# Sixteen delta-memory heads in groups of four instead of two, with feature maps built in place and betas and output weights streamed

## What is computed

```python
# B, S, D = 2, 2048, 256;  H, DK, DV = 16, 128, 128;  SEG = 64 (32 segments)
q, k, v = x @ Wq, x @ Wk, x @ Wv            # x: layer-normed, split in heads and segments
beta = sigmoid(betas)                        # [1, H, 1, DV]
for each segment:                            # carry: mem [B,H,DK,DV], z [B,H,DK,1]
    sigma_q = elu(qq) + 1;  sigma_k = elu(kk) + 1
    att_dot = softmax(causal(qq @ kk.T / sqrt(DK))) @ vv
    att_mem = sigma_q @ mem / (sigma_q @ z)
    delta   = vv - sigma_k @ mem / (sigma_k @ z)
    mem += sigma_k.T @ delta;  z += sum(sigma_k)
    out = (beta * att_mem + (1 - beta) * att_dot) @ Wo
x = x + out
x = x + experts(layernorm(x)) + shared(layernorm(x))
```

## Time and profile before

| | us |
|---|---|
| median of 3 runs (lowest, highest) | 1780.19 (1779.05, 1781.97) |
| the profiled execution, its own time | 1777.83 |
| its span, first to last instruction | 1776.1 |
| TensorE busy | 1719.9 |
| VectorE busy | 1167.2 |
| ScalarE busy | 923.3 |
| GpSimd busy | 534.3 |
| mean granted TensorE clock | 0.996 of full |

### The profile page before, as it was taken

One profiled execution on the slowest core, in us unless ns is written; L12 is line 12 of the kernel. 1 busy time (PEld: TensorE's weight loads), 2 busy tenths in 40 slices (PEclk: granted clock), 3 DMA queues, 4 the chain that ended last, 5 costly groups with the idle time before them and its releaser, 6 DMA issues.

```text
span 1776.1 us, 45751 instructions
## 1 busy us (share of the span) xinstructions
PE 1719.9 (97%) x17966; PEld 1469.0 (83%) x17966; DVE 1167.2 (66%) x4020; ACT 923.3 (52%) x2192; POOL 534.3 (30%) x566
## 2 busy tenths in 40 slices
PE   5899999999999999999999999999999999998998
PEld 5788888888888888888888888888888888885555
DVE  6756757575766757575767757575757767587554
ACT  4655646464655646464646546464646556452130
POOL 2332323232323323232323323232323323230251
PEclk9999999999999999999999999999999999998999
DMA  4200000100000000100000000101000000125947
GB/s 156 72 22 26 15 20 8 33 8 15 26 15 26 16 20 8 33 8 15 26 15 26 16 20 8 33 8 30 11 15 26 15 26 9 30 73 174 293 87 213
DMA packets 83238, 75.07 MB, mean 42 GB/s; under 512 B 21184, under 2 KB 73872, under 8 KB 82768
## 3 DMA queue, kind: packets, MB, share of 16 engines
q1 hardware_dynamic: 79664, 66.32, 12.4%
q0 software_dynamic: 3328, 5.81, 1.7%
q10 hardware_dynamic: 32, 0.01, 0.0%
HBM read 47.72 MB, written 24.40 MB: 41 GB/s over the span
## 4 chain that ended last, share of the span: by engine, by line
PE 90%; DVE 4%; ACT 3%; issue 2%; DMA 1%; SPq 0%; DVEq 0%; ACTq 0%
PE bank_o L1455 13%; PE bank_k L1350 12%; PE bank_q L1350 11%; PE bank_v L1360 9%; PE chain_k L1409 7%; PE chain_k L1399 7%; PE chain_q L1399 6%; PE bank_s L1373 4%; PE bank_a L1426 4%; PE bank_a L1436 3%; PE bank_s L1444 2%; PE bank_k L1382 2%; ACT step_place L657 1%; PE bank_q L1505 1%; PE bank_s L1524 1%
## 5 line engine op out<-in xcount | busy, mean ns | idle before, releaser
L517 POOL TENSOR_TENSOR step_place<-step_place 128x512 f32<-128x512 f32 x128 | 169.8, 1327 | 667.2 <-ACT step_place L657 667.2
L671 ACT ACTIVATE step_place<-chain_q,step_place 128x128 f32<-128x128 f32 x512 | 161.1, 372 | 258.9 <-DVE step_place L903 258.8
L919 DVE TENSOR_TENSOR step_place<-step_place,chain_k 128x258 f32<-128x258 f32 x255 | 107.5, 422 | 277.3 <-PE chain_q L1409 277.3
L1455 PE MATMUL bank_o<-step_place 128*128 128x256 f32 x1024 | 227.8, 381 | 0.9 <-ACT step_place L685 0.9
L1455 PEld LDWEIGHTS bank_o<-step_place 128*128 128x128 f32 x1024 | 193.4, 191 | 26.7 <-issue 1.3
L1409 PE MATMUL chain_k<-step_place 64*128 64x129 f32 x1020 | 180.8, 297 | 2.3 <-DVE step_place L909 2.2
L1409 PE MATMUL chain_q<-step_place 64*128 64x129 f32 x1020 | 180.8, 297 | 0.0
L1399 PE MATMUL chain_k<-step_place 128*64 128x129 f32 x2048 | 165.0, 281 | 10.6 <-DVE step_place L919 10.6
L1409 PEld LDWEIGHTS chain_k<-step_place 64*128 64x128 f32 x1020 | 131.9, 186 | 44.9 <-issue 42.2
L550 POOL TENSOR_TENSOR step_place<-step_place 128x256 f32<-128x256 f32 x128 | 78.5, 613 | 297.4 <-DVE step_place L1112 297.4
L526 POOL TENSOR_TENSOR step_place<-step_place 128x512 f32<-128x512 f32 x128 | 165.4, 1293 | 0.0
(11 more groups left out here) (204 smaller groups left out, 4212.6 us busy)
## 6 DMA issues: line engine op xcount, KB each, us to landing
expert_place<-in_L_ffn_w_dram SPq DMA_DIRECT2D x24, 512.0 KB, 7.5
expert_sums<-zero SPq DMA_DIRECT2D x16, 272.0 KB, 5.1
expert_rows<-w_in SPq DMA_DIRECT2D x15, 288.0 KB, 2.3
step_place<-in_L_attn_x_dram SPq DMA_DIRECT2D x16, 256.0 KB, 2.8
x_res<-in_L_attn_x_dram SPq DMA_DIRECT2D x16, 256.0 KB, 3.2
x_rows<-w_in SPq DMA_DIRECT2D x16, 256.0 KB, 2.1
x_normed_t<-x1t SPq DMA_DIRECT2D x16, 256.0 KB, 2.1
shared_place<-x_normed_t SPq DMA_DIRECT2D x8, 512.0 KB, 4.1
```

Source lines behind the costliest of these rows:

```text
L517: nc.gpsimd.tensor_tensor(vb[:, :, :, :].rearrange("p s j d -> p s (j d)"), val[:, :, :, :].rearrange("p s j d -> p s (j d)"), rows.unsque ...
L671: ins = nc.scalar.activation(am[:, par, seg, j, :], chain_q[:, j * ZC:j * ZC + DK], ACT.Copy, scale=rdq[:, seg, j:j + 1])
L919: ins = nc.vector.tensor_tensor(m, m, (chain_k, chain_q)[b][:, 0:HG * ZC].rearrange("p (j z) -> p j z", j=HG), ALU.subtract)
L1455: ins = mm(bank_o[:, b * D:(b + 1) * D], att[:, b * PIECES + i, :], wo[:, i, :], start=(i == 0 and b == 0), stop=(i == PIECES - 1), skip_g ...
```

## The change

Groups have four heads (HG = 4), so there are four groups in a block and 64 in all. A projection of keys or queries takes two banks (`bank_p[0]`, `bank_p[1]`) of two heads each, and each half has its own semaphore counts; values of one segment are projected with 512 columns into one bank, bank_a for seg 0 and bank_v for seg 1. The fourth head's memory chain does not fit in the banks of the others: it has `chain_3` and, for b = 1 of an update, a piece of `bank_s`. `attend` now has its loops in the order seg, head, b.

The exponentials of keys and queries are written where the feature map will stand, and the feature map is formed in place; betas times values are written where the delta will stand; normalized probabilities overwrite the scores. Only the betas of one group lie in SBUF and only half of Wo (eight pieces): SyncE loads betas once a group and each pair of Wo's pieces in every block, after the pair in its place has been used. Weights land directly where their low parts will be formed, without a landing buffer. The transposes of x, the transposed layer norm, `project_out`, logits and picks use bank_v and bank_a in place of bank_o. `project_out` runs in one piece after `numerators(n, g, 1)` of g = 0. The steps of layer norm and gate are put into four groups in place of eight.

```diff
-HG = 2
+HG = 4
-STEP_PLACE = 23760
+STEP_PLACE = 24545
...
+    def chain(kind, j):
+
+        if j == H3:
+            return chain_3, kind * ZC
+        return (chain_k, chain_q)[kind], j * ZC
+
+    def change(b, j):
+
+        if j == H3:
+            return (chain_3, bank_s)[b][:, 0:ZC]
+        return (chain_k, chain_q)[b][:, j * ZC:(j + 1) * ZC]
...
+        def load_betas(n):
+
+            if n:
+                sp.wait_ge(s["vb_ready"], 2 * n)
...
+        def load_wo(blk, c):
+
+            done = H // WC * (blk - 1) + c + 1 - WR // WC
+            if done > 0:
+                sp.wait_ge(s["wo_used"], done)
...
+            load_betas(n + 1)
             if first:
+                load_x(1)
                 for g in range(2, NG):
                     load_w(g)
...
+                for c in range(WR // WC, H // WC):
+                    load_wo(blk, c)
+                for c in range(WR // WC):
+                    load_wo(blk + 1, c)
+                store_x1(blk)
+                zero_part(blk)
...
         blocks(sp, body)
-        sp.wait_ge(s["v_mm"], NT)
+        for c in range(WR // WC, H // WC):
+            load_wo(NBLK, c)
+        sp.wait_ge(s["v_mm"], 2 * NT)
...
     @block.scalar body:
-                read_out(n, par, 0)
+                read_out(n, 0)
+                if nxt:
+                    for h in range(2):
+                        keys(n + 1, h)
                 act.wait_ge(s["s_shifted"], n + 1)
...
                 if nxt:
-                    queries(n + 1)
+                    for h in range(2):
+                        queries(n + 1, h)
+                if g == 1 and not first:
+                    side_x1t(blk)
+                if g == 2 and not last:
+                    x_turn(blk + 2)
+                read_out(n, 1)
+                if nxt:
+                    values(n + 1, 0)
                 act.wait_ge(s["pt_mm"], n + 1)
...
     @block.vector body:
+                if n:
+                    attended(n - 1)
+                delta(n, 0)
                 dve.wait_ge(s["s_mm"], n + 1)
...
+                if nxt:
+                    sigma_k(n + 1, 0)
+                state_last(n, g, 0)
+                if nxt:
+                    sigma_k(n + 1, 1)
+                state(n, g, 0)
...
+                delta(n, 1, nxt)
+
+                if nxt:
+                    for h in range(2):
+                        sigma_q(n + 1, h)
+                if first and g + 2 < NG:
+                    for i in range(3):
+                        split_lo(g + 2, i)
...
+                if g == 1 and not last:
+                    x_newton(blk + 2, 0, NEWTONS)
+                    x_apply()
                 if g == 2 and not first:
+                    gate_group_sums(blk)
+                    gate_groups(blk)
+                    gate_best(blk)
...
     @block.tensor:
+        def project_v(seg, g):
+            parts = [(w, x, c) for w, x in ((w_hi, xt_hi), (w_hi, xt_lo), (w_lo, xt_hi))
+                     for c in range(NC)]
+            for i, (w, x, c) in enumerate(parts):
+                ins = mm(seg_bank[seg][:, :], x[:, c, seg, :], w[:, g, 2, c, :],
+                         start=i == 0, stop=i == len(parts) - 1)
+            ins.then_inc(s["v_mm"], 1)
...
+            for seg in range(2):
+                pe.wait_ge(s["vo_ready"], 2 * n + seg + 1)
+                if more:
+                    pe.wait_ge(s["v_ready"], 2 * (n + 1) + seg + 1)
                 for j in range(HG):
                     for b in range(B):
...
                         half = b if seg == 0 else 1 - b
-                        ins = mm((bank_a, bank_v)[seg][ROWS[half], j * DK:(j + 1) * DK],
+                        ins = mm(seg_bank[seg][ROWS[half], j * DK:(j + 1) * DK],
                                  pt[ROWS[b], j, seg, :], vo[ROWS[b], seg, j, :],
                                  start=True, stop=True)
...
+                    for h in range(2):
+                        pe.wait_ge(s["ksig_ready"], 2 * n + h + 1)
+                        project_t(h, gn, 1).then_inc(s["k_mm"], 1)
...
+                if n:
+                    attended_transposes(n - 1)
                 update(n, 0)
                 if nxt:
+                    for h in range(2):
+                        pe.wait_ge(s["k_sig"], 2 * (n + 1) + h + 1)
+                        project_t(h, gn, 0).then_inc(s["q_mm"], 1)
...
+                numerators(n, g, 1)
+                if n:
+                    pe.wait_ge(s["att_ready"], 2 * n)
+                if g == 0 and not first:
+                    project_out(blk, n)
...
+                if nxt:
+                    project_v(0, gn)
                 probability_transposes(n)
                 if nxt:
+                    project_v(1, gn)
+                    for h in range(2):
+                        key_transposes(n + 1, h)
...
                 if nxt:
                     update(n, 1)
                 attend(n, nxt)
                 if nxt:
                     scores(n + 1, False)
```

More of the change, by code:

```diff
@@ L179, in layer @@
     kraw = take([128, HG, 2, B, SEG])
-    ex_q = take([128, HG * 2 * B * SEG])
-    ex_k = take([128, HG * 2 * B * SEG])
     val = take([128, 2, HG, DK])
-    vb = take([128, 2, HG, DK])
+    dl = [take([128, HG, ZC]) for seg in range(2)]
     vo = take([128, 2, HG, DK])
@@ L191, in layer @@
     pt = take([128, HG, 2, SEG])
[L192 to L195 removed]
+    am = [take([128, 2, HG, DK]), take([128, 1, HG, DK])]
+    rd = take([128, 2, 2 * HG])
     mask = take([128, SEG])
@@ L547, in body @@
                 nxt = not (last and g == NG - 1)
-                start = first and g == 0
                 pool.wait_ge(s["s_max"], n + 1)
@@ L697, in _ @@
                              ).then_inc(s["gwt_ready"], 1)
-        split_hi(1)
-        keys(0, True)
-        queries(0, True)
-        values(0, True)
-        key_rows(0, True)
+        for seg in range(2):
+            values(0, seg)
+        for h in range(2):
+            queries(0, h)
+        for i in range(3):
+            split_hi(1, i)
+        for h in range(2):
+            key_rows(0, h)
         def body(blk, first, last):
@@ L726, in body @@
-                read_out(n, par, 1)
+                                     bank_s[:, :], ACT.Copy).then_inc(s["pt_ready"], 1)
+                if nxt:
+                    values(n + 1, 1)
                 if first and g + 2 < NG:
-                    split_hi(g + 2)
-                if g == 3 and not first:
-                    side_x1t(blk)
-                if g == 4 and not first:
+                    for i in range(3):
+                        split_hi(g + 2, i)
+                if g == 1 and not first:
@@ L913, in delta, with state_last @@
             ins.then_inc(s["dl_ready"], 1)
+        def state_last(n, g, seg):
+            dve.wait_ge(s["upd_mm"], 2 * n + seg + 1)
+            for b in range(B):
+                m = mem[:, HG * g + H3, b, :]
+                ins = nc.vector.tensor_tensor(m, m, change(b, H3), ALU.subtract)
+            ins.then_inc(s["mem3_ready"], 1)
         def state(n, g, seg):
@@ L1637, in body @@
                     update(n, 1)
+                if g == 1 and not first:
+                    pe.wait_ge(s["lg_exp"], blk)
+                if g == 3 and not first:
+                    pe.wait_ge(s["pickv_ready"], blk + 1)
                 attend(n, nxt)
```

720 lines of the change are left out of this document (358 added, 362 removed).

## The result

| | median us | fast runs against before | 95% interval |
|---|---|---|---|
| before | 1780.26 | | |
| after | 1783.93 (1780.82 to 1788.71) | 1.0022 | 1.0016 to 1.0029 |

The forecast was 1713 us, the range 1652 to 1770. The changed kernel is 4 us slower, by 0.2%, and lies outside the range on the other side of no change.

A forecast was written before the change was run, and what follows sets the result against it. TensorE's instruction stream was the bound. A four-head group at 19.87 us (20.82 for two old) gave start 27, first block 86.3, 14 blocks 1335.6, last 98, rest 162: span 1709, median 1713, range 1652 to 1770.

The forecast's parts named there:

- the extra steps by group: VectorE's added steps in group 2 end at 19.1 us, some 0.3 late a block at most; group 0's residual covered.
- The first block: First block takes 86.3 us (95.20 before): four groups of 19.87, plus 0.4 and 6.4.
- Stage edges (1): TensorE's 1.53 us a group between stages is paid 64 times in place of 128: -98 us.
- Rival D: TensorE's stage edges grow with the heads: +98 us, 1811; chance 0.03.
- Attend (2): Attend's segment-by-segment order keeps two tiles working at a time: +0.87 us a group, +56 us.
- Rival A: TensorE overlaps attend over both segments, as four tiles do before the change: -56 us, 1657; chance 0.10.
- Values (3): Values projection: 12 matmuls of 512 columns at 0.216 us replace 24 of 256: -0.29 us a group, -18 us.
- E: Two row tiles writing one bank take turns in attend, 3.46 us a group: +111 us, 1824; chance 0.02.
- The loop through feature maps: Other engines' chain from numerators to query maps ends at 14.6 us, asked at 14.9: no TensorE wait.
- B: Loop through VectorE and ScalarE costs 0.3 to 1.1 us a group more: 1725 to 1775, middle 1750; chance 0.22.
- C: Loop from numerators to key transposes is 1.4 us or more longer; at 2 us longer, 1822; chance 0.08.
- Streaming of Wo and betas: Reloads are hidden: Wo has 2 us of cover, betas a group's length to land.

The follow-up runs named there:

- light GpSimd steps: Kernel after, with GpSimd's two products of every group touching only 8 of each head's 128 columns; 1704.65 us, 0.9575 of before.
- attend by head: Kernel after, with attend's 32 products ordered head, segment, batch and all waits for values ahead of the first; 1785.78 us, 1.0029 of before.

## Why the prediction failed, step by step

**The failed step: the extra steps by group.** The prediction laid VectorE's steps end to end with their undisturbed durations and found 19.1 in group 2, "some 0.3 late in a block at most"; for group 0 it counted only the residual of 0.7 us and called it covered. In the trace scores wait 2.15 and 1.81 us behind these steps. In group 2 alone L1064 takes 0.89 us more than by itself, L1089 0.68, the low part of x 0.82: 2.4 us. In group 0 the layer norm of x1 behind the residual was no term at all: from the residual to the end of `x1_apply` it is 5.05 us with light GpSimd steps, which costs TensorE nothing, and 7.92 in after, which costs the 1.81. Without GpSimd's long steps both waits are gone and after takes 1704.65 us, 8 below the forecast. That nearness is in part luck: attend was priced 0.39 us a group too high and values 0.17 too low, together 0.9 us a block, which takes the 95.4 of the forecast to the 94.53 of that run. One price in it was also read from the wrong neighbour: the 0.6 us for x's low part rests on steps that read PSUM, while the change moves its operand into SBUF, where the step can be held. And the margin of a few tenths, which the prediction wrote down for two other places, ought to have been asked of these steps too.

**What the 78 us between forecast and span consist of.** Span 1786.9 against 1709: the 14 middle blocks 99.45 us on average in place of 95.4, 56.7 us; the first block about 10, the last about 8 (106.19 for 98), the rest and the start 3. In a middle block the waits are 3.96 us; the lower clock adds 8.9 us over the 14 blocks, and two longer waits 2.3. TensorE's own work is some 0.9 us a block shorter than forecast. That the clock may fall behind a wait was no term of the sum.

**The first block** was forecast at 86.3 us and took 96.07 from numerators to numerators; scores wait 11.8 us in it. With light GpSimd steps it is 88.67, with waits of 7.0: the forecast's 6.4 of lateness was about right. Of the other 7.4 us, 4.8 are waits behind held steps; the remaining 2.6 go with a granted clock of 0.91 in the block, against 0.96.

**Stage edges (1), right.** A group without a wait runs from numerators to numerators in 19.90 us (19.87 forecast):

```profile
899.63 0.86 PE L1500 MATMUL chain_k<-step_place 128*64 128x129 f32 x12
...
919.53 0.72 PE L1500 MATMUL chain_k<-step_place 128*64 128x129 f32 x10
```

Its steady price is 17.76, plus 0.49 for attend, less 0.12 for values, 18.13; a transpose of picks takes 0.11 (the update starts 1.08 us behind the key transposes where it stands between them, 0.97 elsewhere); so the edges come to 1.7 us, about as they did for a group of two heads (1.53), and are paid half as often. Rival D is out.

**Attend (2), right in sign, half in size.** Forecast +0.87 us a group; its order costs 0.48 (94.53 against 92.60 a block). Over 64 groups that would be +31 us in place of +56; the whole kernel showed +23. The step that failed here is "starts stay in program order". The rule of the Trainium skill that stood beside it there, "TensorE: Matmul & The Clock Gate", The mechanism, has starts strictly in order, and for tiled products the rows differ from it: a record starts up to eight places early. Rival A's full overlap holds for eight records a segment and not for sixteen. E is out: attend's 32 records and the edge behind them take 1.52 us (853.04 to the scores at 854.56), not 3.46.

**Values (3), half.** 512 columns take 0.23 us each in after (in the rows below two matmuls lie between 912.12 and 912.58), not 0.216: 12 x (0.24 - 0.23), about -8 us in place of -18.

```profile
912.12 0.63 PE L1457 MATMUL bank_a<-w_hi,xt_lo 128*128 128x512 f32 x2
912.58 0.62 PE L1457 MATMUL bank_a<-w_lo,xt_hi 128*128 128x512 f32 x2
```

**The loop through feature maps, right.** No middle block has a wait of key transposes or of the query projection in after. The result lies between rivals B (to 1775) and C (1822), and both name the right engine, but the loop that they put the lateness into held; it stood in the extra steps of two groups of four. (B's own prices, 0.3 to 1.1 us a group 64 times, give 1732 to 1783 and not 1725 to 1775.) **Streaming of Wo and betas, right:** nothing (1785.75 without it). **In-place writing:** no run takes it alone. With attend and values at their measured prices the block comes to 94.5 us, the 94.53 measured with light GpSimd steps, so nothing is left for it there.

**The price of being slower by 4 us, in one line:** about 75 us of gain on TensorE (1780 to 1705) were made, and 79 us were given back: by VectorE steps held by GpSimd, the waits of scores behind them and the lower clock behind the waits.

## What to carry to other kernels

Before a step is priced on VectorE, lay GpSimd's timeline under it: a step of the kinds held here (two inputs in SBUF, or a copy or `tensor_scalar` in SBUF) lasts to the end of the GpSimd instruction that runs, however small it is, so ask of each moved step which GpSimd instruction it will meet and who is queued behind it. The cure is order first (put what nobody waits for behind the update that TensorE needs: 65 us here) and shorter GpSimd instructions (70 us by itself); the two together with attend's order gave 102 us. Where two segments go to different tiles of TensorE, alternate them within eight records, which are four fp32 products. And count a wait like these of 2.15 to 3.3 us as possibly more than its length, since the clock may fall behind it.

## What the runs showed of the hardware that I had not expected

- VectorE held by GpSimd: an 8-column addition 1.06 us in place of 0.17, ending 0.03 us behind GpSimd's product. A GpSimd product takes 0.29 us for 32 columns, 0.46 for 128 and 1.28 for 512, so cutting the products in four costs GpSimd a third more (440 us for 326) and gives VectorE 72 us back.
- Records of attend's products for a free tile start about eight places ahead of their turn (the second segment's first record 0.50 us behind the first segment's with sixteen records a segment, 0.03 with eight), and a semaphore wait between them makes no difference (1705.05 and 1705.26 us).
- In after the granted clock falls to 1.2 GHz behind three of the 13 waits of 2.15 us in the middle blocks, at the one of 2.94 and the one of 3.29, and behind none of the 13 of 1.81. With attend by head it falls at every wait of group 2 (2.64 us, one of 3.77) and at two of group 0. There the longer waits and the lower clock together took a gain of 4 x 0.49 us a block and more. What decides between the waits of 2.15 us with and without a fall stays open.
